# A decoder layer on one core: ScalarE's six key transfers issued one quarter of a batch later

## The reference

```python
x = x + _L0_attn_ref(_layernorm(x), ...)            # a recurrent mixer over the 100 tokens
x = x + _L0_xattn_ref(_layernorm(x), ctx_768, ...)  # cross attention
x = x + _L0_ffn_ref(_layernorm(x), Wr, W1, W2)      # 8 experts, the best 2 for each token
```

## Time and profile before

| | us |
|---|---|
| three runs, median | 1587.44 |
| lowest, highest | 1583.59, 1594.77 |
| the profiled execution | 1594.53 |
| its span in the profile | 1592.7 |
| TensorE busy in the span | 1350.0 (85%) |
| VectorE busy | 998.6 (63%) |
| GpSimd busy | 799.9 (50%) |
| ScalarE busy | 578.0 (36%) |

### The profile page before, as it was taken

How to read it: one execution, slowest core, us unless ns; L and a number is a source line. 1 busy time by engine, 2 the same in 40 slices (tenths; PEclk the granted TensorE clock), 3 DMA queues, 4 the chain that set the end, 5 groups by cost and what they waited for, 6 DMA issues and landing times. The chain is left out here.

```text
span 1592.7 us, 31746 instructions
## 1 busy us (share of the span) xinstructions
PE 1350.0 (85%) x9914; PEld 906.3 (57%) x9915; DVE 998.6 (63%) x2297; ACT 578.0 (36%) x1420; POOL 799.9 (50%) x1138
## 2 busy tenths in 40 slices
PE   4788778778854899898999898999984799999996
PEld 2455555545543566666666666666652466666664
DVE  2687987787760578787878887788874122222221
ACT  1333323323311345455545555555542122211221
POOL 3234642553344457777767777777764122222222
PEclk9999999999965799999999999999996899999999
DMA  4992000000003666675656676565761232223321
GB/s 147 298 317 80 1 1 1 0 0 1 1 0 71 79 96 111 112 120 108 117 107 121 115 122 115 91 118 112 121 114 40 40 48 45 44 43 46 46 44 23
DMA packets 180331, 128.03 MB, mean 80 GB/s; under 512 B 69010, under 2 KB 173090, under 8 KB 180194
## 3 DMA queue, kind: packets, MB, share of 16 engines
q1 hardware_dynamic: 140242, 94.48, 26.8%
q10 hardware_dynamic: 27648, 17.76, 8.6%
q0 software_dynamic: 12304, 14.10, 5.8%
HBM read 36.10 MB, written 44.83 MB: 51 GB/s over the span
## 5 line engine op out<-in xcount | busy, mean ns | idle before, releaser
L1370 DVE TENSOR_REDUCE neg_raw<-bank_s 100x2 f32<-100x722 f32 x256 | 229.6, 897 | 32.6 <-PE bank_s L1564 32.2
L1241 ACT ACTIVATE prob<-bank_st 120x400 f32<-120x400 f32 (+1 forms) x384 | 166.6, 514 | 166.5 <-PE bank_st L1583 166.5
L1905 POOL DMA_INDIRECT out<-result,target x57 | 88.2, 1548 | 267.2 <-DVE result L1879 264.1
L1381 DVE TENSOR_SCALAR bank_st<-bank_st 120x400 f32<-120x400 f32 (+1 forms) x384 | 196.3, 571 | 0.2 <-PE bank_st L1574 0.2
L751 PE MATMUL bank_l<-q_heads,k 128*100 128x192 f32 (+4 forms) x512 | 121.6, 377 | 62.6 <-DVE attn L565 49.2
L1890 DVE TENSOR_TENSOR hidden<-silu,ebank_v 128x512 f32<-128x512 f32 x57 | 39.2, 688 | 197.3 <-PE ebank_v L1814 197.3
L751 PEld LDWEIGHTS bank_l<-q_heads,k 128*100 128x100 f32 x512 | 80.2, 174 | 111.2 <-DVE attn L565 41.3
L399 ACT ACTIVATE q_heads<-q 32x192 f32<-32x192 f32 (+3 forms) x168 | 62.0, 369 | 223.4 <-DVE q L524 215.0
L1564 PE MATMUL bank_s<-k_st,q_st 96*128 96x361 bf16 x512 | 126.4, 329 | 9.4 <-DVE neg_raw L1370 5.6
L1085 POOL TENSOR_TENSOR neg_diag<-xident_b,neg_max 100x400 bf16<-100x400 bf16 x128 | 109.4, 854 | 48.5 <-DVE neg_max L1375 47.2
L1574 PE MATMUL bank_st<-q_st,k_st 96*128 96x100 bf16 x1536 | 112.3, 213 | 5.9 <-ACT prob L1241 1.1
(11 more groups left out here) (207 smaller groups left out, 2797.8 us busy)
## 6 DMA issues: line engine op xcount, KB each, us to landing
slot_rows<-empty SPq DMA_DIRECT2D x9, 2967.0 KB, 26.6
k_st<-k_part SPq DMA_DIRECT2D x192, 90.2 KB
k_st<-k_part ACTq DMA_DIRECT2D x192, 90.2 KB
q_st<-q_part SPq DMA_DIRECT2D x384, 25.0 KB
kv<-in_ctx_t SPq DMA_DIRECT2D x32, 270.8 KB, 4.9
expert_w<-in_w SPq DMA_DIRECT2D x16, 512.0 KB, 5.1
rows<-slot_rows SPq DMA_DIRECT2D x57, 129.0 KB, 2.0
residual<-in_w SPq DMA_DIRECT2D x16, 256.0 KB, 5.2
```

Source lines behind the costliest of these rows:

```text
L1241: act.activation(prob[0:KEYS[c], t % 2, c], bank_st[c][0:KEYS[c], 0:4 * T], ACT.Exp).then_inc(exp_done, 1)
L1370: dve.tensor_reduce(neg_raw[:, h:h + 2], bank_s[0:T, :, 0:S], AX.X, ALU.max, negate=True).then_inc(max_done, 1)
L1381: dve.tensor_scalar(tile, tile, CLAMP, -CLAMP, ALU.min, ALU.max).then_inc(clipped, 1)
```

## The change

In ScalarE's body, the call of stack_second(b + 1) moves from behind second_row in quarter t = 0 to between the exponentials and norm(b + 2) in quarter t = 1. The six transfers, their waits and their semaphore stay as they are, and so does the call for batch 0 ahead of the loop.

```diff
                     exps(4 * b + t, t)
+                    if t == 1 and more_than(b, 1):
+                        stack_second(b + 1, (b + 1) % 3)
                     if t == 1 and more_than(b, 2):
                         norm(b + 2)
                     if t == 3 and not first:
                         norm3(b - 1, (q - 1) % 4, i if q else i - 1)
                     if t == 0 and routed:
                         second_row(b - 2, (q - 2) % 4)
-                    if t == 0 and more_than(b, 1):
-                        stack_second(b + 1, (b + 1) % 3)
```

## The result

The changed kernel takes 1763.2 us (median of four runs, 1757.2 to 1765.4) against 1586.5 before (the median with a fourth run added to the three above): a ratio of 1.110, 95% interval 1.107 to 1.113, or +177 us. The forecast was 1623, or +36, with a range of 1568 to 1680. The sign was right, and the size was not: the time lies 83 us above the range.

A forecast was written before the change was run, and what follows sets the result against it. TensorE's queue was taken to set the attention stage's pace, so holes in it decide. Late landing 53 + long issue trains 12 + clock 16 - gain 44.5 = +36 us on 1587.4, so 1623 us, range 1568 to 1680.

The forecast's parts named there:

- The gain: First quarter: TensorE's wait for heads_t falls from 38.9 to about 8 us and slow second quarters vanish; both gains 44.5 us.
- The cover on ScalarE: On ScalarE in the second quarter: issues and norm just fit before the third quarter's exponentials; nine long trains cost +12 us.
- The slack of 0.36 us: Before the fourth quarter's exponentials: 0.36 us of each batch's late scores costs nothing, leaving 1.7 of 2.04 us.
- The landing: Keys land 3.0 us after the last issue, 2.04 us late for the next batch's scores; with slack, +53 us in all.
- the signs: What would show it, among others: line 1564 waits for the transfers in nearly every batch, 40 to 70 us in all.
- The clock: TensorE's granted clock falls after the 2 us wait in one batch of three, 10 x 1.6 us: +16 us.
- Rival 3: Clock falls nearly everywhere: landings from e1 (second quarter's first exponential) + 7.5, 25 falls at 2 us: +86 us; chance 0.13.
- Rivals 1 and 2: Rival 1: quick landing, -30 us, 1557, chance 0.14. Rival 2: gain and loss balance, +4 us, about 1593, chance 0.22.

The follow-up runs named there:

- the hole filled: Against the changed kernel, 20 (odd batches: 36) matmuls, overwritten by the scores, put ahead of TensorE's wait for k_st; 1697.4 us.
- three and three: Against the kernel before, three of the six issues stay in the first quarter and three come behind the second quarter's exponentials; 1573.1 us, ratio 0.991.

## Why the prediction was right in sign and wrong in size

1. **The gain** (step "What the change removes"): right. 38.9 us of waits became 7.8, no second quarter runs at half clock, and the kernel without the issues gives 42 us where 44.5 stood.
2. **The cover on ScalarE**: right. Quiet second quarters are 4.62 us with the issues and the norm in them; the mean is 4.91, so trains of issues that run long cost 0.29 x 31 = 9 us, where 12 stood.
3. **The slack of 0.36 us**: right. With the hole filled, the late scores are followed by the exponentials in 3.51 us instead of 3.87 (before).
4. **The landing** (the 3.0 us behind the last issue): this step failed. The landing came 5.6 us behind it in the mean, 4.3 in even batches and 6.9 in odd ones, and TensorE waited 141 us in all, where 63 stood in the sum and 40 to 70 among the signs. With hardly anything beside them the transfers land in 3.3 us, and the wait is then 70 us: so 3.0 was nearly right for transfers that are alone. The error is in their company, which I named ("the residual's store, the next context and, in odd batches, two expert loads") and gave no price. The runs price it: 41 us for the expert weights, 30 for the load and the store, nothing for the scatters. Taking away the queries' transfers from beside the keys, which I counted as relief, brought the bulk loads beside them instead. Nor was it true that the trace shows the landing only by bounds: its events have these very transfers landing 4.6 us behind the last issue in the kernel before. With 4.6 in place of 3.0 the wait in the sum would have been 3.6 us a batch, 113 us in all. The two bounds were also of different worth: the lower one is that of loads in another stage, not in a row of six, and the upper one, 4.4, the shortest of five landings of a like kind.
5. **The clock** ("one batch in three, 10 x 1.6 us"): this step failed too, and mostly by itself. The clock fell in every batch, and cost 72 us where 16 stood. The longer landing explains only part of that: with the bulk transfers moved, the holes are 2.3 us in the mean, close to the 2.04 of the forecast, and the clock falls behind 30 of the 31 and costs 49 us. I read the three waits of the second quarters (3.20 and 1.69 us with a fall, 2.29 without) as a chance of one in three; there, holes of the same length brought the clock down nearly each time, while with three and three it fell behind two of the eight holes of 1.3 to 2.2 us. What decides it besides the length of a hole stays open; no run was made for it. Rival 3 had the mechanism right, and its price of +86 us was put together with a landing at e1 + 7.5 that was again too early (e1 + 9.9).

Rivals 1 and 2 needed a landing within 2.8 us of the last issue; in the run with hardly anything beside the transfers it is 3.3 in the mean (2.2 to 4.3), so neither was to be had at this place in the code. The Trainium skill's fixed 2 us plus bytes (DMA: Bandwidth & Descriptors, "Anatomy of one DMA — SWDGE (gpsimd) path"), an estimate of 2.2 us here, is for one transfer that GpSimd issues, and too low for ScalarE's six in a row: in that same run the last of them lands some 4 us behind the start of its issue. The Trainium skill's sentence in "Issuing engines are not separate DMA queues" on the same page, that DMAs of all engines "run on the same 16 DMA engines and interleave", is what the runs bear out: loads and stores issued by SyncE lengthened TensorE's wait for ScalarE's transfers by 71 us in all.

## What to carry to other kernels

When an issue is moved, look up what other queues issue at the new place, and price it: here the last of six 90 KB transfers landed 3.3 us behind its issue when nearly alone and 6.9 us beside a megabyte of loads. And look for the landing of the very transfers that are moved before taking a bound from others. A hole in TensorE's queue is paid twice if it brings the clock down: here holes of 2.3 and 4.5 us in each batch cost 1.7 and 1.5 times their length. And if a train of issues is in the way at one place and late at the next, it can be split: four here and two there took 1.4% where moving all six lost 11%.

## What the runs showed of the hardware that was not expected

The clock's loss can be bought back by work of no use: 20 or 36 matmuls in each batch, whose result is overwritten, made the kernel 68 us faster, since the work behind the hole ran at 2.4 GHz (a granted clock of 1.00 instead of 0.60 in batch 9's third quarter). Holes of 2.3 us in the mean, one in each batch, were enough to lose it behind 30 of 31. And an issue of a transfer, 0.62 us at the median, was now and then held for 1.2 to 2.2 us on ScalarE's and SyncE's queues at the same time; in the trace of the kernel before, each of the ten issues of ScalarE above 1.2 us in that stage but one began within 0.6 us of the start of an instruction fetch of 16 KB on the DMA engines, of which there was one every 12 us or so. That these holds come from the fetches was not tried.
